# A gated attention and ternary feed-forward kernel: twelve weight chunks stay in their slots, two slots more, and a new order of steps

## What is computed

```python
def _bitlinear(x, w):
    scale = jnp.mean(jnp.abs(w))
    q = jnp.round(jnp.clip(w / (scale + EPS), -1.0, 1.0))
    deq = q * scale
    return x @ deq.T
...
x = x + jnp.tanh(g_xattn[0]) * _L0_xattn_ref(_layernorm(x, axis=-1), ctx_4096, ctx_4096, ...)
z = _layernorm(x, axis=-1)
gate = _bitlinear(z, w_gate)          # w_gate: 2752 x 1024
up = _bitlinear(z, w_up)              # w_up: 2752 x 1024
out = _bitlinear(gate * up, w_down)   # w_down: 1024 x 2752
x = x + jnp.tanh(g_ffn[0]) * out
```

## Time and profile before

| | us |
|---|---|
| median of 3 runs | 1477.16 |
| lowest, highest | 1475.17, 1481.05 |
| the profiled execution | 1473.63 |
| its span | 1471.6 |
| PE busy | 1354.6 |
| DVE busy | 912.6 |
| ACT busy | 646.9 |
| POOL busy | 456.4 |
| mean granted clock of PE, share of full speed | 0.974 |

### The profile page before, as it was taken

One profiled execution on the slowest core, in us unless ns is written; L12 is line 12 of the kernel. 1 busy time (PEld: TensorE's weight loads), 2 busy tenths in 40 slices (PEclk: granted clock), 3 DMA queues, 4 the chain that ended last, 5 costly groups with the idle time before them and its releaser, 6 DMA issues.

```text
span 1471.6 us, 23960 instructions
## 1 busy us (share of the span) xinstructions
PE 1354.6 (92%) x9612; PEld 958.7 (65%) x9612; DVE 912.6 (62%) x1379; ACT 646.9 (44%) x985; POOL 456.4 (31%) x281
## 2 busy tenths in 40 slices
PE   3676698879899999999999999999999999999999
PEld 2454476635577847885587747785577747875884
DVE  6995476668877665766677666766677756621220
ACT  5988766644344333443335333443335333320220
POOL 1379526334633232231323332231323322110000
PEclk9897799989999999999999999999999999999999
DMA  9978997567754454445535463345526543221001
GB/s 351 409 281 304 328 304 176 132 146 162 151 99 101 95 140 96 101 85 118 128 58 116 101 150 80 87 87 129 125 48 116 111 112 79 53 50 58 1 1 43
DMA packets 330158, 195.35 MB, mean 133 GB/s; under 512 B 296064, under 2 KB 296192, under 8 KB 330048
## 3 DMA queue, kind: packets, MB, share of 16 engines
q1 hardware_dynamic: 323136, 168.66, 45.9%
q10 hardware_dynamic: 6912, 25.17, 5.4%
HBM read 103.61 MB, written 16.78 MB: 82 GB/s over the span
## 4 chain that ended last, share of the span: by engine, by line
PE 56%; issue 13%; POOL 12%; DVE 11%; DMA 4%; ACT 3%; POOLq 0%; SPq 0%; ACTq 0%; DVEq 0%
PE ps L794 24%; PE ps L819 16%; PE ps L607 5%; PE ps L608 4%; PE ps L609 4%; POOL qs L1373 3%; POOL ysq L1391 2%; POOL w_dn L1345 2%; DVE q_stat L1247 2%; POOL inter_buf L1345 1%; PE ps L762 1%; POOL xb L1386 1%; DVE q_stat L1231 1%; DMA eT<-p 1%; DVE p L1025 1%
## 5 line engine op out<-in xcount | busy, mean ns | idle before, releaser
L794 PE MATMUL ps<-zT,w_gu 128*128 128x256 f16 x5504 | 627.4, 273 | 9.1 <-DVE gate L1300 6.7
L794 PEld LDWEIGHTS ps<-zT,w_gu 128*128 128x128 fp8e4 x5504 | 539.0, 98 | 92.5 <-DVE gate L1300 8.3
L819 PE MATMUL ps<-w_dn,inter_buf 128*128 128x512 fp8e4 x1376 | 312.2, 380 | 0.4 <-DVE inter_buf L1022 0.4
L1373 POOL TENSOR_TENSOR qs<-qs,q_stat 128x1024 f32<-128x1024 f32 x64 | 126.2, 1971 | 359.4 <-DVE q_stat L1249 359.4
L819 PEld LDWEIGHTS ps<-w_dn,inter_buf 128*128 128x128 f16 x1376 | 134.9, 99 | 156.4 <-issue 2.7
L1300 DVE SCALAR_TENSOR_TENSOR gate<-ps,gate 128x256 f32<-128x256 f32 (+1 forms) x176 | 73.2, 416 | 168.1 <-ACT gate L831 167.5
L831 ACT ACTIVATE gate<-ps 128x256 f32<-128x256 f32 (+1 forms) x176 | 66.3, 377 | 241.5 <-PE ps L794 239.9
L1022 DVE TENSOR_TENSOR inter_buf<-gate,inter_buf 128x256 f16<-128x256 f32 (+1 forms) x176 | 97.6, 554 | 64.9 <-ACT inter_buf L831 64.8
L831 ACT ACTIVATE inter_buf<-gate 128x256 f16<-128x256 f32 (+1 forms) x176 | 72.7, 413 | 110.6 <-DVE gate L1300 110.5
L921 ACT ACTIVATE ek<-ps,kbias,k_unit 128x1024 f32<-128x1024 f32 x64 | 76.8, 1200 | 71.1 <-DVE kbias L1166 61.5
L1379 POOL TENSOR_TENSOR rsv<-ssv,cst 128x4 f32<-128x4 f32 x32 | 36.8, 1151 | 222.7 <-DVE ssv L1265 222.7
(11 more groups left out here) (139 smaller groups left out, 1912.1 us busy)
## 6 DMA issues: line engine op xcount, KB each, us to landing
w_dn<-in_down_w SPq DMA_DIRECT2D x22, 512.0 KB, 5.1
inter_buf<-in_gate_w SPq DMA_DIRECT2D x20, 512.0 KB, 7.8
inter_buf<-in_up_w SPq DMA_DIRECT2D x20, 512.0 KB, 7.0
w_dn<-in_up_w SPq DMA_DIRECT2D x20, 512.0 KB, 6.0
w_dn<-in_gate_w SPq DMA_DIRECT2D x19, 512.0 KB, 9.1
xb<-in_x ACTq DMA_DIRECT2D x16, 512.0 KB, 4.2
x_dram<-xb SPq DMA_DIRECT2D x16, 512.0 KB, 3.0
fin<-x_dram SPq DMA_DIRECT2D x32, 256.0 KB, 3.4
```

The costliest lines, as they stand in the source:

```text
L794: last = nc.tensor.matmul(ps[:, j % 2, s * T:s * T + T], w_gu[:, w, k, :], zT[:, h, k, :], start=(k == 0 and h == 0), stop=(k == NC - 1 an ...
L819: mm = nc.tensor.matmul(ps[:, hf, :], lhs, w_dn[:, j, hf * 512:hf * 512 + 512], start=(u == 0), stop=(u == total - 1))
L1373: nc.gpsimd.tensor_tensor(v, v, q_stat[:, u % 2, 1, :].unsqueeze(2).broadcast_to([P, 2 * HEADS, DH]), ALU.mult).then_inc(q_prob, 1)
```

## The change

It alters five things.

1. The first six chunks of gate and of up (`STAY = (6, 6, 0)`) are summed last and stay in their slots until they are rounded; they are not loaded a second time. Down chunks are all loaded twice as before. Since the sum may not destroy what stays, ACT's `Abs` of such a chunk writes to scratch (`k16`, f16), and `kf_hi` of image 2, the first that writes `k16` for the attention, waits for all sums of gate and up.
2. Both thresholds of gate and up wait for all sums of both (`wpart_`).
3. 13 slots instead of 11: `stage_c` holds slots 11 and 12.
4. ACT sums 14 and DVE 8 of the 22 chunks of a matrix instead of 16 and 6.
5. All tables of the order are new, and all eight groups have tables of their own. The leads of second loads are 10.5 to 40.8 us for gate and up (before 4.2 to 19.3) and 5.2 to 21.7 us for down (before -2.6 to 28.5: some loads were planned to be used before their slot was free). In the new order group 0 has the planned start 169.2 instead of 148.9 us, and more attention of images 2 and 3 stands before it. `ld_xr` gets a wait for `x2_stored`.

The diff, cut to its core (of the tables two lines):

```diff
-FFN_FROM = (1489, 3382, 5019, 6625)
-EVERY = 1606
...
+FFN_FROM = (1692, 3397, 5096, 6699, 8305, 9911, 11517, 12861)
...
+STAY = (6, 6, 0)
+
+
+def stays(kind, m, c):
+
+    return kind == "wquant" and c < STAY[m]
+
+
+def summed_in_order(m):
+
+    return [("wsum", m, c) for c in (*range(STAY[m], J), *range(STAY[m]))]
+
+
+SUMS = [s for m in (GATE, UP) for s in summed_in_order(m) if s[2] >= STAY[m]]
+SUMS += [("wsum", m, c) for c in range(STAY[GATE]) for m in (GATE, UP)]
...
-SUM_ACT = [c for c in range(IC) if c % 5 != 0]
+SUM_ACT = [c for c in range(IC) if c % 3 != 0]
+ACT_SUMS = [s for s in SUMS + DOWN_SUMS if s[2] in SUM_ACT]
...
-STAGES = 11
+STAGES = 13
...
-        rounds_down = kind == "wquant" and m == DOWN
-        fits = [s for s in range(STAGES)
-                if (s > 4 or USED[n] + 20 < FFN_FROM[0] + GU_AT[0][8 * s])
-                and not (4 < s < 10 and rounds_down and c >= J - 40 + 4 * s)]
-        s = min(fits, key=lambda s: last[s])
+        if stays(kind, m, c):
+            s = slots[STAGE_OF["wsum", m, c]]
+        else:
+            until = USED[n] if kind == "wquant" or c >= STAY[m] else USED[STAGE_OF["wquant", m, c]]
+            rounds_down = m == DOWN and (kind == "wquant" or c < STAY[m])
+            fits = [s for s in range(STAGES)
+                    if (s > 4 or until + 20 < FFN_FROM[0] + GU_AT[0][8 * s])
+                    and not (4 < s < 10 and rounds_down and c >= J - 40 + 4 * s)
+                    and s not in staying.values()]
+            s = min(fits, key=lambda s: s if m == DOWN and kind == "wsum" and c < STAY[m] else last[s])
...
-        at.append((-90 if BEFORE[n] < 0 else USED[BEFORE[n]], "wload", (m, c, n)))
+        if not stays(kind, m, c):
+            at.append((-90 if BEFORE[n] < 0 else USED[BEFORE[n]], "wload", (m, c, n)))
...
             def ld_xr(i, _):
+                wait(act, x2_stored, 16 * (i - 1))
...
-                nc.scalar.activation(v, v, ACT.Abs, accum_out=absum[:, m, c:c + 1]).then_inc(wsum_act, 1)
+                w = v
+                if c < STAY[m]:
+                    kept = [q for q in ACT_SUMS if q[2] < STAY[q[1]]]
+                    k = kept.index(("wsum", m, c))
+                    if k > 1:
+                        act.wait_ge(wsum_act, ACT_SUMS.index(kept[k - 2]) + 1)
+                    if m == DOWN:
+                        act.wait_ge(ct_lo_s, BY_PE)
+                    w = ct_raw[:, :].bitcast(F16)[:, k % 2 * CH:k % 2 * CH + CH] if m == DOWN else k16[:, k % 2, :]
+                nc.scalar.activation(w, v, ACT.Abs, accum_out=absum[:, m, c:c + 1]).then_inc(wsum_act, 1)
...
             def kf_hi(i, p):
+                if i == BY_PE and p == 0:
+                    act.wait_ge(wsum_act, 2 * len(SUM_ACT))
...
-                dve.wait_ge(wsum_act, (m + 1) * len(SUM_ACT))
-                dve.wait_ge(wsum_dve, (m + 1) * (J - len(SUM_ACT)))
+                dve.wait_ge(wsum_act, max(m + 1, 2) * len(SUM_ACT))
+                dve.wait_ge(wsum_dve, max(m + 1, 2) * (J - len(SUM_ACT)))
```

More of the change, by code:

```diff
@@ L205, in planned @@
-def planned(kind, i):
-    if i < 4 * GB:
-        return PLAN[kind][i]
-    return [group_start(i // GB - 1) + t for t in PLAN[kind][4 * GB + i % GB]]
+    "ld_ctx": [[], [152], [640], [1199], [1627], [2440], [3043], [3859], [4800], [5648], [6414], [7225], [8048],
+        [8831], [9654], [10437]],
+    "cabs": [[48], [443], [857], [1368], [1719], [2487], [3103], [3912], [4877], [5706], [6471], [7294], [8123],
+        [8900], [9729], [10506]],
+    "csum": [[60], [531], [891], [1409], [2159], [2990], [3820], [4756], [5598], [6368], [7179], [8000], [8785],
+        [9606], [10391], [11212]],
@@ new lines @@
+    "ktr": [[241, 432, 518, 567], [770, 920, 998, 1041], [], [], [], [], [], [], [], [], [], [], [], [], [],
+        []],
+    "k_hi": [[262, 444, 530, 579], [788, 938, 1012, 1057], [], [], [], [], [], [], [], [], [], [], [], [], [],
+        []],
+    "k_lo": [[350, 468, 555, 603], [811, 950, 1028, 1073], [], [], [], [], [], [], [], [], [], [], [], [], [],
+        []],
+    "kf_hi": [[], [], [1310, 1428, 1524, 1639], [1846, 2231, 2362, 2485], [2572, 2895, 2995, 3105], [3238, 3492,
[3 rows of a table added]
+    "kf_lo": [[], [], [1339, 1442, 1537, 1651], [1859, 2243, 2375, 2499], [2594, 2920, 3008, 3123], [3284, 3504,
[3 rows of a table added]
@@ L212, in attention_times @@
+QUANT_AT = [763, 775, 787, 798, 809, 821, 832, 849, 909, 955, 966, 977, 989, 1000, 1022, 1052, 1077, 1088, 1099,
[3 rows of a table added]
+SIGN_AT = [777, 811, 861, 872, 884, 917, 928, 977, 988, 1022, 1034, 1045, 1067, 1090, 1103, 1142, 1154, 1166,
[3 rows of a table added]
+SMALL_AT = {"lmax": [31, 60, 93], "lsum": [38, 108, 114], "lscale": [43, 113, 119], "l_hi": [48, 123, 130],
+    "l_lo": [67, 138, 161], "prod": [76], "gains": [105]}
 def attention_times(i):
@@ L215, in attention_times @@
     for kind in PLAN:
-        for n, t in enumerate(planned(kind, i)):
+        for n, t in enumerate(PLAN[kind][i]):
             a = (n // PAIRS, n % PAIRS) if kind == "outp" else (n,)
@@ L222, in ffn_times @@
 def ffn_times(g):
-    start, at = group_start(g), []
-    gu, down = GU_AT[min(g, 3)], DOWN_AT[min(g, 3)]
+    start, gu, down, at = FFN_FROM[g], GU_AT[g], DOWN_AT[g], []
     for n, t in enumerate(gu):
@@ L238, in ffn_times @@
     return at
-SUMS = [("wsum", m, c) for m in (GATE, UP) for c in range(J)]
+STAY = (6, 6, 0)
[5 more added lines that the diff above has]
+SUMS += [("wsum", m, c) for c in range(STAY[GATE]) for m in (GATE, UP)]
 QUANTS = [("wquant", m, c) for c in range(J) for m in (GATE, UP)]
-DOWN_SUMS = [("wsum", DOWN, c) for c in range(J)]
+DOWN_SUMS = summed_in_order(DOWN)
 DOWN_QUANTS = [("wquant", DOWN, c) for c in range(J)]
@@ L429, in staged @@
             n = STAGE_OF[step]
-            loads = [STAGED[k] for k in range(n + 1) if SLOT[k] == SLOT[n]]
+            loads = [STAGED[k] for k in range(n + 1) if SLOT[k] == SLOT[n] and not stays(*STAGED[k])]
             return SLOT[n], 16 * (len(loads) + loads.count(("wquant", DOWN, IC)))
```

212 lines of the change are left out of this document (113 added, 99 removed), and 142 rows, old and new, of tables (DOWN_AT, GU_AT, PLAN, QUANT_AT).

## The result

The changed kernel takes 1431.7 us (median of 4 runs, 1431.16 to 1433.92), the kernel before 1478.16 us beside it: a ratio of 0.9705, with a 95% interval of 0.9682 to 0.9728. That is faster, as forecast, but the 1431.7 us lie 17.3 us under the predicted 1449 and 2.3 us under the low end of the range (by the ratio, on the 1477.16 us of the forecast, 1433.6, just under 1434). The interval of the ratio is 1430.2 to 1437.0 us, so it isn't settled on which side of 1434 the time lies. The profiled execution took 1432.09 us, with a span of 1430.1.

The account below looks back on a forecast made before the run. POOL's queue was taken to bound the start of group 0, PE the stretch from group 1: 179.8 + (231.8 - 18.2 - 31) + 1082.6 = 1445.0 us span, plus 2.0 gives 1447.0; against 1450.5 by the median, 1449 was taken, range 1434 to 1474.

Parts of the forecast that it names:

- PE bounds the last stretch: From group 1 to the end only PE's own work counts; 6.4 us of moved work make 1076.2 us 1082.6.
- rival 1: The order buys more: group 0 at 176 us, 36 of 43 us back, last stretch shorter; about 1437 us, chance 0.13.
- Moved work and first rounding: PE work: 11.8 us more before group 0, 18.2 less in the middle, 6.4 more after; first rounding at 85.8 us.
- POOL up to group 0: POOL's full queue sets group 0's start: 2.2 us later rounding plus 14.0 us more work, 163.6 to 179.8 us.
- rival 3: Before group 0, DVE work beside the gate roundings slows them: 9 us, total 1458 us, chance 0.05.
- rival 2: ACT bounds the start of group 0, as its chains don't pack: 188 us, total 1457 us, chance 0.05.
- Twelve chunks that stay, at nothing: Twelve fewer second loads of gate and up, 21 us of transfers, gain nothing, since POOL's own work covers them.
- Down slots, 31 us: Group 0 to group 1: slots 11 and 12 end down-load waits; 31 us return, 7.5 from the clock; bounds 0 and 40.
- POOL's waits for down loads: Sign to look for: these waits, 43.0 us between 223 and 305 us before the change, fall under 10 us.
- The last `Sign`: Sign to look for: the last `Sign` into w_dn comes before 287 us, against 304.8 before the change.
- Rival 4, transposes: Between first and last down rounding, more loads in flight slow transposes: 14 us, total 1463 us, chance 0.05.
- Rival 6, SP's queue: Transposes among gate and up second loads delay loads on SP, starving POOL before group 0: 42 us, 1491 us, chance 0.05.

## Why the prediction was right in direction and low in size

**PE bounds the last stretch: the step that failed.** "Here only PE's own work counts; nothing that the change does to loads or rounding can shorten it." The second half was true and beside the point, since the change also gives the later groups new tables. The moved work was sized rightly: PE's steps there add up to 1057.8 us before and 1064.3 after, +6.5 against the 6.4 of the sum. But 14.5 us of the 1076.2 were idle, and 3.7 are left. The sum kept all the lost time of this stretch, so it put the effect of the new tables there at nothing. By the count above, lost time fell from 18.4 to 3.8 us: 10.8 of the 14.6 are PE's idle time, and the rest stood in its records as busy time beyond the steps' usual durations. The run with the old later tables in the new kernel puts these tables at 19 us of the whole time, a part of which is the join, and the reverse run at 16 (11.9 us of the last stretch in its profile). Without the 14.5 us by which this stretch missed, the span would have been 1444.6, close to the 1445.0 of the sum. That closeness is partly luck: the first two stretches missed by +4.5 and -4.9 us, which cancel. I had seen the larger leads, and rival 1 had the last stretch lose "some of the 14 us", but at 0.13. Of that rival's three parts two came true, this one at its full size and "36 of the 43 us" in the middle (35.9); the third, group 0 at 176 us, did not.

**Moved work and first rounding.** PE's steps up to group 0 grew from 65.9 to 77.8 us, 11.9 for the 11.8 of the sum, and those of the middle stretch shrank from 188.4 to 170.1, 18.3 for 18.2. The first rounding came at 84.7 us for 85.8. All three were right.

**POOL up to group 0**: z of image 1 at 179.4 for 175, group 0 at 184.3 for 179.8. From first rounding to z POOL was busy for 71.4 us before and for 89.1 after, 17.7 for the 14.0 of the sum. The missing 3.7 us are covered by slower roundings, (1.196 - 1.130) x 43 = 2.8, and by `x2a`, 4 x (1.507 - 1.267) = 1.0: the mechanism of rival 3 at under half of its price. Its idle time went from 4.2 to 5.6 us, and that part is not POOL's: it shrinks to 2.5 when k has two buffers. So "POOL's queue sets that start" was only a part of it: with seven roundings taken off POOL the start moved by only 0.6 us. ACT was busy for 85.13 of 99.6 us, 85%, and its chains didn't pack, which is rival 2 in small.

**Twelve chunks that stay, at nothing**: 3.7 us by the medians, of which 0.5 before group 0. The cover that I named (POOL's own work) was there. What it gave was in the middle stretch.

**Down slots, 31 us**: the middle stretch lost 43.4 us before and 7.5 after, so 35.9 came back, 4.9 more than the sum and within its bound of 40. Of the two parts, PE's idle time was the one sized too low: it fell from 31.4 to 3.9 us (177.7 - 173.8), 27.5 for the 23.5 of the sum. The clock, 0.98 for 0.95, gave (1 - 0.95) x 231.8 - (1 - 0.98) x 177.7 = 8.0 us for 7.5. The mechanism was right: slots alone recovered 22, and going back to 11 in the kernel in which nothing stays cost 17.6, of which 7.7 in the middle. POOL's waits for down loads were to be under 10 us and were 1.8. The last `Sign` came 5 us later than I said, but PE no longer waited for anything behind it.

**Rival 4, transposes**: their landing did get longer, 13.3 us for the `kT` issued at 181.82, where the kernel before has 11.8 at most, and 15.1 us for the `cT` issued at 132.2. In the middle stretch PE hardly waited for them. Their price fell before group 0, on ACT and by way of a buffer, where I had not looked.

**Rival 6, SP's queue**: the transpose at 181.82 held SP for 11.37 us, behind which stood down loads:

```profile
181.82 11.37 SPq L649 DMA_TRANSPOSE kT<-k  x1
```

Its sign, POOL idle for second loads before group 0, is absent (0.0 us). The leads of 10 us and more covered it, as the prediction held against it.

## What to carry to other kernels

A stretch in which the bounding engine is 98.7% busy still holds what its 1.3% are worth over its length: sum its short waits by releaser before calling the stretch fixed, above all when the change rewrites its order. Cost every part of a change that replaces a table, also where its headline is about something else: here the later tables and the split of the sums weighed more than the chunks that stay. And when work is taken off the engine that looks full and its start doesn't move, look for a single buffer in a neighbour's queue, behind which that start waits.
